# Graph layer on one core: x added by the transfers that load it, in the node stage

## The reference

```python
h = maximum(layernorm(x), 0)
msg = relu(h[src] + edge)                 # 25000 x 256
p = msg @ W.T + b                         # 25000 x 256
scores = p @ Q.T                          # 4 heads
alpha = softmax of scores over the edges of one destination
pooled[n, h] = sum over edges of n of alpha[:, h] * p
gate = softmax(mean over edges of n of p @ Wg.T + bg)
out = x + sigmoid(sum over h of gate[n, h] * pooled[n, h])
```

## Time and profile before

| | us |
|---|---|
| median of 3 runs | 654.74 |
| lowest and highest | 654.54, 656.39 |
| span of the profiled execution | 732.9 |
| first sigmoid of the node stage, in the span | 411.1 |
| last store issued, in the span | 729.7 |

### The profile page before, as it was taken

The page is one execution under the profiler, slowest core; times in us unless marked ns, Lnnn a source line. Parts: engine busy times, 40 slices in busy tenths (PEclk is TensorE's granted clock), DMA queues, the critical chain, the costliest instruction groups (busy, mean ns, idle before and its releaser), DMA issues.

```text
span 732.9 us, 12416 instructions
## 1 busy us (share of the span) xinstructions
PE 548.9 (75%) x2474; PEld 434.1 (59%) x2475; DVE 487.6 (67%) x1644; ACT 383.3 (52%) x661; POOL 453.4 (62%) x339
## 2 busy tenths in 40 slices
PE   2417988878779868879403998888888778877785
PEld 2205876666558656758202876776667566665564
DVE  4208678788879768769798766666565655555555
ACT  2105455656457545647211254666666666666674
POOL 7765565665560656550053366777877887778785
PEclk9999899999999999989855999999999999999999
DMA  7434455555553468775300799999999999999999
GB/s 223 131 93 134 147 173 174 165 174 154 174 170 114 129 224 271 237 234 191 115 0 1 247 355 383 314 307 329 357 319 329 325 327 339 325 337 336 341 333 332
DMA packets 137238, 171.53 MB, mean 234 GB/s; under 512 B 10096, under 2 KB 123784, under 8 KB 137202
## 3 DMA queue, kind: packets, MB, share of 16 engines
q10 hardware_dynamic: 91344, 90.23, 37.6%
q1 hardware_dynamic: 33010, 42.70, 18.6%
q0 software_dynamic: 12848, 38.20, 16.5%
HBM read 111.50 MB, written 59.60 MB: 233 GB/s over the span
## 4 chain that ended last, share of the span: by engine, by line
PE 52%; issue 12%; ACT 11%; DVE 10%; another core or an unknown queue 5%; ACTq 4%; DVEq 3%; POOL 2%; DMA 2%; POOLq 0%; SPq 0%
PE bank L745 24%; PE bank L829 18%; PE bank L735 7%; ACT arena L597 5%; DVE spread L1248 3%; ACT bank L573 3%; POOL arena L478 2%; ACTq L600 2%; DVEq L1252 1%; ACT arena L505 1%; ACTq L552 1%; ACTq L605 1%; ACT arena L497 1%; DMA p_keep<-p_spill 1%
## 5 line engine op out<-in xcount | busy, mean ns | idle before, releaser
L829 PE MATMUL bank<-p_keep,spread 128*128 x1172 | 274.1, 388 | 51.6 <-DVE spread L1248 46.7
L829 PEld LDWEIGHTS bank<-p_keep,spread 128*128 128x128 f32 x1172 | 219.0, 192 | 107.5 <-issue 79.8
L1248 DVE TENSOR_SCALAR spread<-bank,rel,wgt 128x128 f32<-128x128 f32 x586 | 195.8, 404 | 128.5 <-PE bank L829 72.8
L478 POOL TENSOR_TENSOR arena<-arena 128x1024 f32<-128x1024 f32 x96 | 224.9, 2352 | 73.1 <-ACT arena L597 72.7
L745 PE MATMUL bank<-w_all,arena 128*128 128x264 f32 (+1 forms) x784 | 228.0, 417 | 53.2 <-ACT arena L505 40.2
L745 PEld LDWEIGHTS bank<-w_all,arena 128*128 128x128 f32 (+1 forms) x784 | 143.7, 204 | 78.9 <-ACT arena L505 50.9
L597 ACT ACTIVATE arena<-bank 128x1024 f32<-128x1024 f32 x97 | 99.2, 1023 | 139.3 <-PE bank L829 120.3
L443 POOL DMA_INDIRECT p_keep<-in_x_dram,idx x124 | 120.8, 975 | 72.6 <-issue 31.5
L505 ACT ACTIVATE arena<-bank 128x256 f32<-128x256 f32 x196 | 73.6, 376 | 124.2 <-PE bank L735 71.0
L443 POOL DMA_INDIRECT arena<-in_x_dram,idx x72 | 70.1, 973 | 64.7 <-ACT arena L497 33.7
L573 ACT ACTIVATE bank<-zero 128x1024 f32<-128x1024 f32 x98 | 100.5, 1026 | 3.0
(11 more groups left out here) (202 smaller groups left out, 190.6 us busy)
## 6 DMA issues: line engine op xcount, KB each, us to landing
out_dram<-arena ACTq DMA_DIRECT2D x97, 512.0 KB, 4.5
arena<-in_x_dram ACTq DMA_DIRECT2D x73, 512.0 KB, 5.4
arena<-in_edge_attr_dram SPq DMA_DIRECT2D x48, 512.0 KB
arena<-in_x_dram POOLq DMA_DIRECT2D x24, 512.0 KB, 5.8
p_spill<-p_keep SPq DMA_DIRECT2D x16, 512.0 KB
p_keep<-p_spill SPq DMA_DIRECT2D x16, 512.0 KB, 5.8
p_keep<-in_x_dram,idx POOLq DMA_INDIRECT x124
arena<-in_x_dram,idx POOLq DMA_INDIRECT x72
```

What stands on the lines that cost most here:

```text
L478: pool.tensor_tensor(yout[:, slot, :, :], yout[:, slot, :, :], xin[:, slot, :, :], ALU.add).then_inc(summed, 1)
L829: nc.tensor.matmul(places[:, bass.ds(place, T)], spread[:, k0 + k, :], p_rows[:, bass.ds(p_at, T)], start=False, stop=True, skip_group_che ...
L1248: v.tensor_scalar(spread[:, k, :], bank[:, 7, P:2 * P], rel[:, bass.ds(s0 + k, 1)], wgt[:, bass.ds(s0 + k, 1)], ALU.is_equal, ALU.mult).th ...
```

## The change

In the node stage POOL issues all transfers of x and of the output. When a group's sigmoid is in its slot, POOL issues a transfer of x whose destination is that slot, with the operation `add`: the transfer adds x to what the slot holds. Two groups later (`STORE_LAG`) POOL waits until that transfer has landed and issues the store. ACT keeps the sigmoid and the zeroing only, and no engine adds. The four x slots become four more result slots, so there are eight (`YS = 8`). The four early loads of x are gone. POOL's loop over the groups is written out, ACT's loop has a period of 24 groups instead of 12. The tail's additions on DVE are gone too.

```diff
-    XS, YS = 4, 4
-    PERIOD = 12
+    YS = 8
+    STORE_LAG = 2
+    PERIOD = 24
...
-        xin = arena[:, 0:XS * GROUP * D].rearrange("p (s q d) -> p s q d", s=XS, q=GROUP)
-        yout = arena[:, XS * GROUP * D:(XS + YS) * GROUP * D].rearrange("p (s q d) -> p s q d", s=YS, q=GROUP)
+        yout = arena[:, 0:YS * GROUP * D].rearrange("p (s q d) -> p s q d", s=YS, q=GROUP)
...
-            def add_four(g0, first, more):
-                for slot in range(4):
-                    pool.wait_ge(sig_done, g0 + slot + 1)
...
-                    pool.tensor_tensor(yout[:, slot, :, :], yout[:, slot, :, :], xin[:, slot, :, :],
-                                       ALU.add).then_inc(summed, 1)
-                    if slot in more:
-                        pool.wait_ge(summed, g0 + slot + 1)
-                        pool.dma_start(xin[:, slot, :, :], x_later[:, bass.ds((g0 + slot + XS) * GROUP, GROUP), :]
-                                       ).then_inc(x_pool[slot], 16)
...
+            def add_x(g, slot):
+                pool.wait_ge(sig_done, g + 1)
+                pool.dma_start(yout[:, slot, :, :], x_rows[:, g * GROUP:(g + 1) * GROUP, :], accum_op=ALU.add
+                               ).then_inc(x_added[slot], 16)
+
+            def store(g, slot, times):
+                pool.wait_ge(x_added[slot], times)
+                pool.dma_start(o_rows[:, g * GROUP:(g + 1) * GROUP, :], yout[:, slot, :, :]).then_inc(stored[slot], 16)
+
+            for g in range(FULL + STORE_LAG):
+                if g < FULL:
+                    add_x(g, g % YS)
+                if g >= STORE_LAG:
+                    store(g - STORE_LAG, (g - STORE_LAG) % YS, 16 * ((g - STORE_LAG) // YS) + 16)
...
             act.wait_ge(ln_done, TILES)
-            for g in range(XS):
-                load_x(g, g)
...
                     act.wait_ge(sig_done, g + 1)
                     clear(k % SLOTS)
-                    store(g - 1, (k - 1) % YS)
-                    if (k + 3) % XS not in BY_POOL:
-                        load_x(g + 3, (k + 3) % XS)
...
-            slot = (FULL - 1) % 4
-            dve.wait_ge(sig_done, FULL)
-            dve.wait_ge(x_pool[slot], 16 * ((FULL - 1) // 4))
-            v.tensor_tensor(yout[:, slot, :, :], yout[:, slot, :, :], xin[:, slot, :, :], ALU.add).then_inc(last_summed, 1)
```

More of the change, by code:

```diff
@@ L94, in gnn_layer @@
     LAST_WHOLE = (N - FULL * GROUP * P) // P
-    XS, YS = 4, 4
-    PERIOD = 12
+    YS = 8
+    STORE_LAG = 2
+    PERIOD = 24
     ROUNDS = FULL // PERIOD
-    BY_POOL = (0,)
-    assert FULL % 4 == 1 and (FULL - 1) % 4 in BY_POOL
-    assert PERIOD % SLOTS == 0 and PERIOD % XS == 0 and LAST_WHOLE == 2 and N % P and FULL % PERIOD == 1
+    assert FULL % YS == 1
+    assert PERIOD % SLOTS == 0 and PERIOD % YS == 0 and LAST_WHOLE == 2 and N % P and FULL % PERIOD == 1
     scratch = nc.dram_tensor("p_spill", [SPILL // 4 * P, 4 * T], F32).ap()
@@ L158, in gnn_layer @@
         RW = BLK * P
-        o = XS * GROUP * D
+        o = 4 * GROUP * D
         run = arena[:, o:o + C * RW].rearrange("p (k e) -> p k e", k=C); o += C * RW
@@ L290, in gnn_layer @@
         reloaded = [sem("reloaded0"), sem("reloaded1")]
-        sig_done, summed, last_summed = sem("sig_done"), sem("summed"), sem("last_summed")
-        x_in = [sem(f"x_in{k}") for k in range(XS)]
-        x_pool = [sem(f"x_pool{k}") for k in range(XS)]
+        sig_done = sem("sig_done")
+        x_added = [sem(f"x_added{k}") for k in range(YS)]
         stored = [sem(f"stored{k}") for k in range(YS)]
@@ L467, in _ @@
             pool.tensor_tensor(tot[:, 0, :], tot[:, 0, :], tot[:, 1, :], ALU.add).then_inc(by_first_done, 1)
-            x_later = x[0:FULL * GROUP * P, :].rearrange("(t p) d -> p t d", p=P)
-            def add_four(g0, first, more):
-                for slot in range(4):
-                    pool.wait_ge(sig_done, g0 + slot + 1)
[L474 to L477, removed]
-                    pool.tensor_tensor(yout[:, slot, :, :], yout[:, slot, :, :], xin[:, slot, :, :],
-                                       ALU.add).then_inc(summed, 1)
-                    if slot in more:
-                        pool.wait_ge(summed, g0 + slot + 1)
-                        pool.dma_start(xin[:, slot, :, :], x_later[:, bass.ds((g0 + slot + XS) * GROUP, GROUP), :]
-                                       ).then_inc(x_pool[slot], 16)
@@ L485, in _ @@
[L485 to L488, removed]
+            x_rows = x[0:FULL * GROUP * P, :].rearrange("(t p) d -> p t d", p=P)
+            o_rows = out[0:FULL * GROUP * P, :].rearrange("(t p) d -> p t d", p=P)
+            last_row = (FULL * GROUP + LAST_WHOLE) * P
+            def add_x(g, slot):
+                pool.wait_ge(sig_done, g + 1)
+                pool.dma_start(yout[:, slot, :, :], x_rows[:, g * GROUP:(g + 1) * GROUP, :], accum_op=ALU.add
+                               ).then_inc(x_added[slot], 16)
@@ new lines, in store @@
+            def store(g, slot, times):
[6 more added lines that the diff above has]
+                    store(g - STORE_LAG, (g - STORE_LAG) % YS, 16 * ((g - STORE_LAG) // YS) + 16)
+            slot = FULL % YS
+            pool.wait_ge(sig_done, FULL + 2)
@@ new lines, in _ @@
+            pool.dma_start(yout[:, slot, 0:LAST_WHOLE, :],
+                           x[FULL * GROUP * P:last_row, :].rearrange("(t p) d -> p t d", p=P), accum_op=ALU.add
+                           ).then_inc(x_added[slot], 16)
+            pool.dma_start(yout[0:N % P, slot, LAST_WHOLE, :], x[last_row:N, :], accum_op=ALU.add
+                           ).then_inc(x_added[slot], 16)
+            pool.wait_ge(x_added[slot], 16 * (FULL // YS) + 32)
+            pool.dma_start(out[FULL * GROUP * P:last_row, :].rearrange("(t p) d -> p t d", p=P),
+                           yout[:, slot, 0:LAST_WHOLE, :]).then_inc(stored[slot], 16)
@@ L490, in _ @@
+            pool.dma_start(out[last_row:N, :], yout[0:N % P, slot, LAST_WHOLE, :]).then_inc(stored[slot], 16)
+            for k in range(YS):
+                pool.wait_ge(stored[k], 16 * len(range(k, GROUPS, YS)) + (16 if k == slot else 0))
         @block.scalar
@@ L546, in _ @@
                     copy_rows(step_tile[:, 2 * PART:STEPS], 5)
-            x_rows = x[0:FULL * GROUP * P, :].rearrange("(t p) d -> p t d", p=P)
-            def load_x(g, slot):
-                act.dma_start(xin[:, slot, :, :], x_rows[:, bass.ds(g * GROUP, GROUP), :]).then_inc(x_in[slot], 16)
             act.wait_ge(ln_done, TILES)
-            for g in range(XS):
-                load_x(g, g)
             act.wait_ge(keep_turned, 1)
@@ L581, in _ @@
             act.wait_ge(wgt_ready, 1)
[L582 to L590, removed]
             def places(z, n):
@@ L601, in steps_of @@
                 return word & 1023, (word >> 10) & 1023, word >> 20
[L603 to L610, removed]
             for k in range(PERIOD):
@@ L619, in _ @@
                 clear(k % SLOTS)
[L620 to L623, removed]
             with act.Fori(1, ROUNDS - 1) as r:
@@ L643, in _ @@
                     clear(g % SLOTS)
[L644 to L648, removed]
             slot = FULL % YS
@@ L655, in _ @@
                                  ACT.Sigmoid).then_inc(sig_done, 1)
[L656 to L662, removed]
         @block.tensor
```

## The result

| | us |
|---|---|
| before, median of 5 runs (lowest, highest) | 655.3 (654.5, 661.2) |
| changed, median of 5 runs (lowest, highest) | 745.8 (742.6, 763.4) |
| ratio, 95% interval | 1.133 (1.126 to 1.139) |
| predicted | 772 (685 to 880) |

The change costs 90 us where 117 were forecast. The ratio is of the three lower executions of the changed kernel; the profiled one took 762.9 us, one of two slower ones among the five, so its numbers are those of an execution 17 us above the median.

What follows compares the result with a forecast made beforehand. The prediction took transfers, at about 328 GB/s, to bound the node stage. Three passes, 1.34 + 2 x 1.46 = 4.26 us a group, put the span 119 us later; 654.7 + 119 was rounded to 772 us, range 685 to 880.

Steps and rivals of the forecast that it cites:

- The fetch of the old content: Node stage: an adding load also fetches the slot's old 512 KB, one further pass of 1.34 us a group.
- The other two passes: Node stage: loading x and storing the output on POOL's queue at 360 GB/s, 1.46 us a pass.
- the prediction's own sum: Span end: first sigmoid's end at 412, 97.66 groups of 4.26 us (416), 19 loads back, 5 tail: 852 us.
- The prediction's own lower bound: Node stage with all three passes at 392 GB/s: span ends at 827 us, +94.
- the upper bound of +175: Node stage with all three passes at 328 GB/s: span ends at 412 + 468 + 23 + 5 us.
- the reading of the DMA share: Node stage before: a DMA share of 1.01 read as full use, so transfers bound it at about 328 GB/s.
- The count of bytes: Node stage before: 191.3 transfers of 1.60 us, 306 us, put the span's end at 737 us; it was 732.9.
- the rival of the engines: Node stage: old bytes are free and engines are the bound; 619 or 643 us, faster at chance 0.10.
- ACT's relief: Node stage: ACT loses about 0.7 us of issues a group; no gain while transfers bound, otherwise up to 51 us.
- POOL's issues: Node stage: two issues a group, accumulating one 0.77 to 1.54 us, no bound; rival that they bound: 876 us, chance 0.02.
- The port lock: POOL's issues: DVE instructions may lock POOL out while it writes descriptors; at 3.1 us an issue, stage 605 us; judged unsupported.
- The wait: POOL's program: three loads share one landing, period (landing + 1.1 us) / 3; 2.3 us at a 5.8 us landing, bounding nothing.

Runs made afterwards that it cites:

- The additional loads: Changed kernel plus one more load of x a group into two spare slots that nothing reads: plain 866.2 us, accumulating 1000.6 us.
- SP's queue above: Kernel before with SP issuing ACT's stores and loads from the twelfth group on, and POOL's loads too: 639.9 us, 0.976 of the kernel before.
- the longer lag: Changed kernel with STORE_LAG 4 instead of 2: executions of 742.7 to 797.5 us, the two lower ones at ratio 1.136 to the kernel before.
- with plain loads: Changed kernel with plain instead of accumulating loads, so x overwrites the sigmoid: 660.3 us, ratio 1.008 to the kernel before.
- the run where they had POOL's queue to themselves: Changed kernel with stores issued by ACT, four groups behind, and POOL issuing accumulating loads alone: 786.3 us, ratio 1.200 to the kernel before.

## Why the prediction was right, and where its sizes were not

**The fetch of the old content** was taken as one further pass at 1.34 us. The additional loads show one pass, 1.39 us. This price also holds what smaller packets cost, since an accumulating load goes in packets of 1 KB and POOL's plain load in larger ones; no run has one without the other. An estimate bounds that part: a pass in packets of 1 KB took 1.46 us at most (SP's queue above) and the plain additional load 1.24, so the packets are 0.22 us or less of the 1.39, and the fetch the rest. The Trainium skill ("Collectives: The Full Stack", "The bandwidth ceiling: the fold count and why AG ≠ RS ≠ AR") has an adding transfer read two sources, and measured a ratio of 1.93 between ring steps without and with an addition. Here it is (1.24 + 1.39) / 1.24 = 2.1, so these runs agree, with a surcharge a little larger.

**The other two passes** are the term that was mis-sized: 1.46 us each, from the share of POOL's queue, against 1.24 measured for one additional plain load, 43 us over 97.66 groups. The price of a store was not measured by itself; the sum here takes the same. With the measured prices a group is 1.39 + 2 x 1.24 = 3.87 us, and the prediction's own sum gives 332 + 378 + 19 + 5 = 734 for a first sigmoid that ends at 332; the three runs near the median had spans of 741 to 744, so by this sum a group took 3.96 us, not 4.26, and 7 to 10 us stay without a cause. The prediction's own lower bound, all passes at 392 GB/s, was +94, and the measured +90 lies just under it. Three of its figures do not follow from its terms: 654.7 + 119 is 774 and not 772; +94 makes 749, where the chances begin the range at 740; and the upper bound of +175 counts the loads back as 23 us, where 8.4 MB at 328 GB/s, less the 4 us ahead of the stage, are 22.

**The step behind it that failed** is the reading of the DMA share. "The bytes that a busy DMA engine moves are the same with and without a crowd" made 328 GB/s a ceiling. It was not: with a load added the same engines carried some 400, at a share of 1.14, and the kernel before with SP issuing moved its own bytes at 360. The count of bytes that came out at 737 for 732.9 fitted only because 328 was taken from the stage itself. So the chain of before, which gave DMA 2%, was nearer to the truth than the forecast allowed, and the rival of the engines was right in half: the engines did hold the stage before, but the old bytes are not free, and three passes, 3.9 us, exceed the 3.2 us that the engines need. Two, 2.5 us by the same price, do not.

**ACT's relief** was costed at nothing, because transfers would hide it. That is right for this change, since its transfers became the bound. In the kernel before, moving those issues to SP was worth 8 us.

**POOL's issues** are 1.30 us for an accumulating load, inside the bounds of 0.77 and 1.54, and were off the path: POOL was busy for 50 of 100 us. The port lock of the Trainium skill ("SBUF — State Buffer", "Who interferes with whom") did not show: the longest of these issues took 1.47 us. **The wait** behind the landing came as described, landing 11.3 us for "some 12" and (11.3 + 1.1) / 3 = 4.1 us, but the longer lag shows it to be a consequence. The forecast that ACT's sigmoid would wait for `stored` did not show in the first profile after, where PE's waits ended last; it did in the second, with 100.8 us, and with the longer lag.

**The clock** was given no cost. It did fall, to 0.88 in 600 to 700 us; with transfers as the bound that cost nothing that the runs show.

## What to carry to other kernels

Here an addition made by a transfer was not free: it cost the transfer engines about one pass more. It pays only where the transfer engines have a third pass to spare, which is asked at the rate they can reach and not at the rate that they show. A full DMA share beside compute engines with hand-overs between them proves no ceiling; add a transfer that nothing reads, or leave a part of one out, and see what it costs. When an engine is relieved of issuing, give the issues to an idle one before giving it other work.

## What was not expected of the hardware

- The DMA share is no gauge of a limit: 0.99 at 338 GB/s with plain loads, 1.01 at 329 before, and 1.14 at 303 that with the fetch are 404.
- Accumulating loads moved in small packets. In the run where they had POOL's queue to themselves 23,997 packets carried 23.83 MB, 1 KB each; in the kernel before POOL's plain loads had 3.6 KB.
- An accumulating issue takes 1.30 us of POOL where a plain one takes 0.77.
- PE's granted clock was lower where it was kept waiting longer: 0.98 before, with PE busy for 83 of 100 us; 0.81 with the additional plain load, 64 of 100; 0.72 with the additional accumulating load, 58 of 100. These are means between its levels of 1.2 and 2.4 GHz. In the edge stage it had been 1.00 with 6 of 20, so the busy share of a window does not tell it by itself.
